# Bias and causal mask of two attentions in 32-key steps and 32-wide blocks, on one Trainium2 core

## What is computed

```python
# layer 0, 16 heads of width 8, 256 queries and keys
buckets = _relative_position_bucket(mem_pos - ctx_pos)   # 0 for keys after the query,
bias = rel_bias[buckets]                                 # up to 31, reached some 30 keys back
scores = einsum('bqhd,bkhd->bhqk', q, k) / sqrt(dh) + transpose(bias, (2, 0, 1))[None]
context = einsum('bhqk,bkhd->bqhd', softmax(scores), v)
# layer 1
att = where(causal, einsum('bthd,bshd->bhts', q, k) / sqrt(D), -inf)
y = einsum('bhts,bshd->bthd', softmax(att), v) @ w_proj + b_proj
```

## Time and profile before

| | us |
|---|---|
| median of the timed runs | 3942.99 |
| profiled execution | 3959.12 |
| its span, first to last instruction | 3956.8 |
| TensorE busy (matmuls) | 3403.3 (86%) |
| VectorE busy | 2900.9 (73%) |
| ScalarE busy | 1902.9 (48%) |
| GpSimd busy | 1549.3 (39%) |
| mean granted TensorE clock | 0.942 |

### The profile page before, as it was taken

One profiled execution on the slowest core, in us unless ns is written; L12 is line 12 of the kernel. 1 busy time (PEld: TensorE's weight loads), 2 busy tenths in 40 slices (PEclk: granted clock), 3 DMA queues, 4 the chain that ended last, 5 costly groups with the idle time before them and its releaser, 6 DMA issues. The chain is left out here.

```text
span 3956.8 us, 60602 instructions
## 1 busy us (share of the span) xinstructions
PE 3403.3 (86%) x20989; PEld 2093.9 (53%) x21044; DVE 2900.9 (73%) x6458; ACT 1902.9 (48%) x3463; POOL 1549.3 (39%) x1015
## 2 busy tenths in 40 slices
PE   5999999878999984677748888888886999999987
PEld 3677776555777762344423333333333666666653
DVE  7888888556777756433239999999997777777765
ACT  2555556324665651222237676776673333333325
POOL 2311111542211200588848877878873011111112
PEclk9999999999999996799869999999998999999998
DMA  6333332004444424233332332322321222222211
GB/s 154 94 89 90 88 89 54 1 5 115 100 101 104 98 62 122 57 44 44 43 78 73 95 100 83 93 78 73 95 79 60 90 87 87 87 87 87 88 59 43
DMA packets 242530, 314.19 MB, mean 79 GB/s; under 512 B 46450, under 2 KB 157779, under 8 KB 231588
## 3 DMA queue, kind: packets, MB, share of 16 engines
q1 hardware_dynamic: 208308, 289.02, 26.3%
q0 software_dynamic: 22528, 17.32, 3.3%
q10 hardware_dynamic: 11392, 3.97, 0.5%
HBM read 251.93 MB, written 57.08 MB: 78 GB/s over the span
## 5 line engine op out<-in xcount | busy, mean ns | idle before, releaser
L574 DVE TENSOR_REDUCE a_Mx<-a_Sx 128x2 f32<-128x512 f32 (+1 forms) x1024 | 590.3, 618 | 172.2 <-PE a_Sx L626 126.7
L2208 POOL TENSOR_TENSOR a_inp<-a_dtu,a_Bs 128x1024 f32<-128x1024 f32 x256 | 597.8, 2359 | 67.9 <-DMA a_Bs<-a_brows 42.5
L2486 DVE TENSOR_TENSOR_SCAN a_h<-a_dA,a_inp 128x1024 f32<-128x1024 f32 x256 | 583.0, 2283 | 31.7 <-ACT a_dA L2369 27.2
L2613 PE MATMUL a_Y<-a_hc,g_ident 128*128 128x512 f32 x1024 | 487.8, 599 | 7.4 <-POOL a_hc L2222 3.5
L347 POOL TENSOR_TENSOR a_rest<-a_qk,a_parts 128x512 f32<-128x512 f32 x64 | 75.2, 1175 | 916.1 <-ACT a_parts L399 916.1
L413 ACT ACTIVATE a_Pr<-a_SA 128x512 f32<-128x512 f32 x512 | 305.4, 596 | 168.6 <-DVE a_SA L524 79.6
L623 PE MATMUL a_Sx<-att_Kp,att_Qp 96*128 96x256 bf16 (+1 forms) x2048 | 345.3, 261 | 42.7 <-DMA att_Qp<-a_crows 17.9
L2369 ACT ACTIVATE a_dA<-a_dtA,a_A 128x512 f32<-128x512 f32 x512 | 329.8, 681 | 97.5 <-DVE a_h L2486 96.5
L1958 ACT ACTIVATE f_sg<-f_GB 128x512 f32<-128x512 f32 x272 | 162.6, 598 | 436.6 <-PE f_GB L2034 436.4
L2084 PEld LDWEIGHTS f_OUT<-g_routed_wd,f_hm 128*128 128x128 f32 x2176 | 280.6, 191 | 123.5 <-issue 90.5
L2613 PEld LDWEIGHTS a_Y<-a_hc,g_ident 128*128 128x128 f32 x1024 | 195.4, 194 | 234.2 <-issue 223.0
(11 more groups left out here) (480 smaller groups left out, 6771.3 us busy)
## 6 DMA issues: line engine op xcount, KB each, us to landing
a_Bs<-a_brows SPq DMA_DIRECT2D x256, 256.0 KB, 3.3
f_Cs<-f_crows SPq DMA_DIRECT2D x512, 128.0 KB, 2.9
att_Qp<-a_packing SPq DMA_DIRECT2D x192, 192.0 KB
att_Kp<-a_packing SPq DMA_DIRECT2D x192, 192.0 KB
a_packing<-a_parts SPq DMA_DIRECT2D x64, 384.0 KB
a_packing<-a_parts SPq DMA_DIRECT2D x64, 128.0 KB
a_Cs<-a_brows SPq DMA_DIRECT2D x32, 256.0 KB, 4.7
g_x<-x SPq DMA_DIRECT2D x8, 512.0 KB, 7.3
```

The source lines that it names most:

```text
L574: nc.vector.tensor_reduce(Mx[(k + 2 - (j < LATE)) % 2][:, t, 2 * jj:2 * jj + 2], Sx[t][:, 0:2 * wd].rearrange("p (h q) -> p h q", h=2), AX ...
L2208: nc.gpsimd.tensor_tensor(inp[n % Q][:], dtu[k][:], Bs[n % Q][:].unsqueeze(1).to_broadcast([P, CH, GT]), ALU.mult).then_inc(s["mulB"], 1)
L2486: nc.vector.tensor_tensor_scan(h[n % 2][:].rearrange("p c q -> p (c q)"), dA[m % 2][:].rearrange("p c q -> p (c q)"), inp[n % Q][:].rearra ...
L2613: nc.tensor.matmul(Y[c][:], ident[:], hc[n % Q][:, c], start=False, stop=(n == N - 1))\
```

## The change

In the first attention the far bias becomes a step per 32 keys: the six constant rows become 24 (eight blocks of 32 keys by three parts), filled straight from the stored lines. What is left of the bias then lies in blocks of 32 queries by 64 keys around the diagonal, and is added at all four places by four matmuls that write 32 partitions each (`fold`, 96 x 32, stationary; `near_q` or `near_k` moving, 128 columns, twice 64 at the border). `add_band`, `band`, `bmax`, `bexp` and their TensorE and VectorE setup go; the lines shrink from 3 x 512 to 768 columns, and all placing moves to SP, ahead of the packing's second half. In the causal attention the 24 rows hold -1e30 for keys in later blocks of 32, and the mask inside a block is added by four matmuls of 2 x 32 columns at each of the four places. Each small matmul increments the semaphore, whose waits count by W = 4. In `choose` four matmuls of 512 columns whose result nobody reads follow the matmul of each of 30 rounds. In `state_space` `spread_C` for n = 3 and 6 is issued one state earlier, ahead of the `Y` matmuls of n = 1 and 4.

```diff
@@ attention, SP @@
+                        if not causal and b == -3:
+                            bias.store(sp)
@@ after the two packing stores of the step @@
+                        if not causal and b == -3:
+                            bias.place(sp)
+                            constants(0, s["consts"])
@@
                     if not causal and b == -3:
-                        bias.store(sp)
-                        constants(0, s["consts"])
                         constants(1, s["consts"])
@@ attention, ScalarE @@
-                            wait(act, s["sa_mm"] if causal else s["biased"], 8 * b + j + 1)
+                            wait(act, s["sa_mm"], W * (8 * b + j + 1))
@@ attention, VectorE @@
-                def add_band(b, j):
-                    v.wait_ge(s["sa_mm"], 8 * b + j + 1)
-                    near = pair(SA[j % 2], K0Q)[:, :, 0:BAND]
-                    nc.vector.tensor_tensor(near, near, band[:, 2 * j:2 * j + 2], ALU.add).then_inc(s["biased"], 1)
@@ attention, TensorE @@
+                def add_mask(both, mask, done):
+                    for r in range(4):
+                        tile = slice(32 * r, 32 * r + 32)
+                        nc.tensor.matmul(both[tile, :, tile], identb[:, tile],
+                                         mask[:, tile].unsqueeze(1).to_broadcast([P, 2, 32]),
+                                         start=False, stop=True).then_inc(done, 1)
@@ maxima @@
                         if causal:
-                            last = nc.tensor.matmul(both[:, :, wd - P:wd], identb[:],
-                                                    maskq[:].unsqueeze(1).to_broadcast([P, 2, P]), start=False, stop=True)
+                            add_mask(both[:, :, wd - P:wd], maskq, s["mx_mm"])
                         else:
-                            last = nc.tensor.matmul(both[:, :, lo:hi], flip[:], bmax[...], start=False, stop=True)
+                            for r in range(4):
+                                q0 = t * P + 32 * r
+                                lo = max(q0 - 32, 0)
+                                nc.tensor.matmul(both[32 * r:32 * r + 32, :, lo:q0 + 32], fold[:],
+                                                 near_q[:, 2 * j:2 * j + 2, lo - q0 + 32:64],
+                                                 start=False, stop=True).then_inc(s["mx_mm"], 1)
+                def add_bias(both, h0, first_key, done):
+                    for r in (3, 0, 1, 2):
+                        q0 = first_key + 32 * r
+                        hi = min(q0 + 64, S)
+                        nc.tensor.matmul(both[32 * r:32 * r + 32, :, q0:hi], fold[:], near_k[:, h0:h0 + 2, 0:hi - q0],
+                                         start=False, stop=True).then_inc(done, 1)
@@ scores_near: add_mask(both[:, :, 0:P], ...) or add_bias(both, h0, 0, s["sa_mm"]); scores_far: @@
-                        for i in range(NPART):
-                            last = nc.tensor.matmul(both[:, :, P:2 * P], flip[:], bexp[:, i, h0:h0 + 2, 0:P],
-                                                    start=False, stop=(i == NPART - 1))
+                        add_bias(both, h0, P, s["sb_mm"])
@@ choose, TensorE, b in range(BITS + 1) @@
+                for i in range(BESIDE if b < BITS else 0):
+                    nc.tensor.matmul(IDLE[:], identb[:], identb[:].unsqueeze(1).to_broadcast([P, BL, P]),
+                                     start=True, stop=True)
@@ state_space, TensorE @@
-                    if on(0) and n < N - 1 and n + 1 not in MOVED:
+                    if on(0) and n < N - 1 and n not in MOVED and n + 1 not in MOVED:
                         spread_C(g * N + (n + 1), n + 1, k)
@@
                         wait_product(pe, g * N + n)
+                        if n + 1 in MOVED:
+                            spread_C(g * N + (n + 2), n + 2, k)
```

More of the change, by code:

```diff
@@ L558, in step @@
                         bb, jj = slot(b, j)
[L559 to L569, removed]
                         if (x_ if j >= LATE else m):
                             for t in range(TB):
-                                wait(v, s["mx_mm"], 16 * bb + (2 * jj + t + 1))
+                                wait(v, s["mx_mm"], W * (16 * bb + (2 * jj + t + 1)))
                                 wd = P * (t + 1) if causal else S
@@ L639, in scores_near @@
                     for u in range(2):
-                        last = nc.tensor.matmul(both[:, u], K[:, h0 + u, 0:P], Q[:, h0 + u, :],
-                                                start=(u == 0), stop=(u == 1 and not causal))
+                        nc.tensor.matmul(both[:, u], K[:, h0 + u, 0:P], Q[:, h0 + u, :],
+                                                start=(u == 0), stop=False)
                     if causal:
-                        last = nc.tensor.matmul(both[:, :, 0:P], identb[:],
-                                                maskk[:].unsqueeze(1).to_broadcast([P, 2, P]), start=False, stop=True)
-                    last.then_inc(s["sa_mm"], 1)
+                        add_mask(both[:, :, 0:P], maskk, s["sa_mm"])
+                    else:
+                        add_bias(both, h0, 0, s["sa_mm"])
                 def scores_far(b, k, j):
@@ L748, in step @@
                             pe.wait_ge(s["thr_ready"], 2)
-                            pe.wait_ge(bias.band_placed, NPART * 16)
-                            for g, hs in enumerate(BANDS):
-                                wait(pe, s["band_ev"], g - 1)
-                                for i in range(NPART):
-                                    last = nc.tensor.matmul(
-                                        SA[g % 2][:, 0:len(hs) * BAND].rearrange("p (h q) -> p h q", q=BAND),
-                                        flip[:], bexp[:, i, hs[0]:hs[-1] + 1, :],
-                                        start=(i == 0), stop=(i == NPART - 1))
-                                last.then_inc(s["band_mm"], 1)
                         if x_ and j == LATE:
@@ L822, in store @@
     def store(self, sp):
[L823 removed]
         sp.wait_ge(self.seq, 5)
[L825 to L828 removed]
+        sp.dma_start(self.lines.rearrange("i h n -> h i n"), self.lparts[:]).then_inc(self.stored, 16)
     def place(self, eng):
@@ L840, in look_up @@
     def look_up(self, pe):
         pe.wait_ge(self.loaded, 32)
-        for i in range(3):
-            self.nc.tensor.matmul(self.LP[i], self.rel[:], self.hot[:, i, :], start=True, stop=True)\
-                .then_inc(self.made, 1)
+        for out, cols in self.LP:
+            self.nc.tensor.matmul(out, self.rel[:], self.hot[:, cols], start=True, stop=True).then_inc(self.made, 1)
     def copy_lines(self, act):
-        N, line = self.N, self.line
-        act.wait_ge(self.made, 3)
-        for i in range(3):
-            self.nc.scalar.activation(line[:, i * N:i * N + N], self.LP[i], ACT.Copy).then_inc(self.got, 1)
+        act.wait_ge(self.made, 2)
@@ L2651, in l1_attn @@
     norm_factors(nc, res, "n2")
-    attention(nc, res, "a2", {"zrows": a["c_zrows"]}, True, res["held"])
+    attention(nc, res, "a2", {"later": a["c_later"]}, True, res["held"])
 def l0_ffn(nc, res, a):
```

130 lines of the change are left out of this document (57 added, 73 removed).

## The result

| | before | after |
|---|---|---|
| median of the timed runs, us | 3943.31 (4 runs) | 4117.01 (4 runs, 4113.69 to 4117.43) |
| profiled execution / its span, us | 3959.12 / 3956.8 | 4117.43 / 4115.2 |
| busy: TensorE / VectorE / ScalarE, us | 3403.3 / 2900.9 / 1902.9 | 3627.0 / 2809.4 / 1925.6 |
| a batch, first / causal attention, us | 19.71 / 17.30 | 22.23 / 20.36 |

The change makes the kernel slower: ratio 1.044, 95% interval 1.0421 to 1.0458, or +174 us.

What follows compares the result with a forecast made beforehand. The prediction took TensorE's stream to bound both attentions. First attention +75, causal +89, start-up -16, search -5 and recurrence 0 made +143 us, put on the 3943.0 median: 4086 us, range 4025 to 4165.

Steps and rivals of the forecast that it cites:

- The bound: Both attentions: TensorE's stream sets the time, busy 541 of 555 us and 466 of 480; relieving VectorE is worth little.
- The price of a layout change: Small groups in both attentions: 0.095 us each way, so a group costs 0.265 us in the first, 0.24 in the second.
- A batch: Attention batches grow by 2.35 us in the first and 2.78 in the second; times 32, +75 and +89 us.
- What TensorE's gaps gave back: Waits in TensorE's stream that the longer stream fills: 0.8 us recovered a batch in the first attention.
- Start-up: Before the first attention's scores: the expanded-bias wait and band making go (14 us), -16 us in all (-22 to -6).
- the first is shorter too: Start-up: TensorE's 17.9 us wait for the constant rows, until 44.55, was also to become shorter.
- The search: Search for the k-th score: four idle matmuls a round lift the clock from 0.50, -5 us (-9 to +10).
- The recurrence: Earlier spread of C for n = 3 and 6: gain eaten by a later wait, 0 us (+3 to -15).
- (a): Rival on the attentions' small groups: no layout price, -151 us, some 3800 us in total; chance 0.10.
- (b): Rival on the attentions' small groups: half the layout price, 85 us less in each stage, about 3935 us; chance 0.05.
- (c): Rival on TensorE in the attentions: granted clock falls to 0.95, adding 67 us, 4155 us in total; chance 0.08.
- (d): Rival on the small matmuls: they run one after the other, adding 170 and 90 us, about 4350 us; chance 0.04.

Runs made afterwards that it cites:

- two-trips run: Changed kernel, reordered so that TensorE enters the small-matmul layout twice a pair of heads instead of four times; 3947.36 us, ratio 1.0008 to the kernel before.
- warm start: Changed kernel plus seventy idle 512-column matmuls on TensorE ahead of its wait for the constant rows; 4120.87 us, ratio 1.0456 to the kernel before.
- run `ordinary`: Changed kernel with each small group as four ordinary matmuls, stationary operands zero-padded to 128 columns; 3988.69 us, ratio 1.0113 to the kernel before.

## Why the prediction came out as it did

It said 4086 us and a range of 4025 to 4165; 4117 is inside it, 31 above the forecast. Step by step:

- **The bound.** Right. TensorE's stream sets the length of a batch; 3.9 us less work for VectorE a batch bought nothing beyond the gaps.
- **The price of a layout change.** Right. It forecast 0.20 in and 0.15 out, a group at 0.265 and 0.24; the trace has 0.202 and 0.161 (0.135 for 64 columns), a group at 0.263 and 0.237. That the price is for changing the layout and not for the small matmuls is shown by the two-trips run. What the prediction did not have: the second ordinary matmul behind a group starts 0.119 after the first in place of 0.109. With 32 groups that is 0.3 us a batch.
- **A batch.** +2.35 forecast, +2.53 measured; +2.78 forecast, +3.06 measured. The 0.3 above covers both differences. What TensorE's gaps gave back, taken as the remainder, was right in size: in the first attention 3.13 + 0.32 - 2.53 = 0.9 us (0.8 forecast), in the causal one 3.43 + 0.32 - 0.1 (the groups being 0.003 cheaper each) - 3.06 = 0.6 (0.65 forecast). Times 32: +81 and +98 for +75 and +89, so 15 us of the miss.
- **Start-up.** Wrong, the largest single miss: -16 forecast (-22 to -6), some -4 measured. Up to the ternary layer the changed kernel is 77 us behind the first profile of the kernel before, 75 behind the later one, and 32 batches make 81. The band and its wait did go. The first scores of the kernel before, then TensorE in the changed kernel:

```profile
76.56 0.60 PE L640 MATMUL a_SA<-att_Qp,att_Kp 128*128 128x256 bf16 x4
```

```profile
45.96 0.61 PE L614 MATMUL a_Sx<-att_Kp,att_Qp 96*128 96x256 bf16 x2 [19.71 <-DMA att_Qp<-a_lines]
...
71.02 0.61 PE L639 MATMUL a_SA<-att_Qp,att_Kp 128*128 128x256 bf16 x2
...
81.86 0.59 PE L614 MATMUL a_Sx<-att_Kp,att_Qp 96*128 96x256 bf16 x2
82.37 0.24 PE L622 MATMUL a_Sx<-a_near_q,a_fold 96*32 96x64 bf16 x4
82.55 0.39 PE L614 MATMUL a_Sx<-att_Kp,att_Qp 96*128 96x256 bf16 x2
```

  The first maxima start at 45.96 for 44.55: the wait is longer (19.71 for 17.90), not shorter, and it is a DMA that fills the `Qp` rows from the lines. And the maxima that follow run at half speed, two of 256 columns in 0.61 us for 0.39, until 82 us. The kernel before is at half speed to 48.7 us and again, while it mostly waits for the expanded bias, from 58.9 to 69.2. So the first scores come at 71.02 for 76.56, 5.5 us earlier and not 15, and the batch that they begin lasts 25.6 us for 18.9, 6.7 longer, where a steady one is 2.5 longer. The two failed steps are "the first is shorter too" and the unstated assumption that what follows runs at full speed.

  What the half speed costs was to be shown by the warm start, which could not hold the clock. The run `ordinary` tells more. It has the same sums and the same constant rows, and its clock rises at 53.4 us:

```profile
53.40:63.60 10.20, 8.45 (x83) 6.01 (x82) 9.23 (x17) 2.23 (x5) 3.46 (x3) 1.00 0.61 105
63.60:67.00 3.40, 3.40 (x24) 2.83 (x22) 2.54 (x6) 1.28 (x1) 0.00 (x0) 0.50 0.57 159
67.00:82.00 15.00, 14.89 (x198) 12.47 (x197) 9.71 (x21) 8.84 (x18) 3.44 (x3) 1.00 0.50 115
```

  Its first scores start at 67.98, and its ternary layer 38.5 us later than before, where 32 batches, 1.50 longer each, make 48: its start-up is shorter by 9.5 us, against 4 in the changed kernel. That puts the half speed at some 5 us, an estimate, for layout changes in the filling batches are in it too; 6 or 7 us of the forecast's 16 are missing even there. In all seven profiles with the small groups in the first attention these matmuls come to full speed between 79.7 and 87.7 us, in the six without them by 53.4 (with one spell at 0.50 after it). So the long half speed comes with the small groups; how they keep the clock low is open.
- **The search.** -5 forecast; from the first to the last count 5.5 less in the changed kernel and alone; a round takes 1.75 us for 1.95 once the clock has risen.
- **The recurrence.** 0 forecast; from the first scan to the last 946.2 us for 947.0 (944.1 and 944.9 in the other profiles of the kernel before), and 1.000 alone.
- **The sum.** +81 + 98 - 4 - 5.5 = +169 for the measured +174 (+171 between profiles of like expert-choice layers). Putting the forecast's difference on the median, and not on the profiled execution's 3959, was right; its 16 us above the median lay for 10 us in the expert-choice layer.
- **The rivals.** (a) no layout price: excluded by the rows above. By the Trainium skill's page "TensorE: Matmul & The Clock Gate", section "Packing small matmuls — row/col tiling", the small matmuls start about 4 ns apart, and the trace agrees with 3. It doesn't charge the coming and going: 28 more entries and exits a batch, at 0.093 + 0.106, are 5.6 us, more than the whole loss of 2.5 or 3.1. (b) half the price: excluded by 0.202 and 0.161 together. (c) a lower clock: 1.00 in both windows; it was low in the start-up alone. (d) in series: 0.003 from one to the next.

Of the signs that it named, those for the distances (0.15 and 0.20), the batches (22 and 20), and the search's clock (0.95, above 0.9) came, and TensorE's gaps shrank; VectorE's share fell to 66% and not to 60%; the first scores came 5.5 us earlier and not 15.

## What to carry to other kernels

Count the changes of TensorE's tile layout before the columns: each costs some 0.09 us in and 0.10 out, together the time of some 450 columns of ordinary streaming (256 in 0.109), so a group of small matmuls side by side pays only if it replaces more than that and its own stream, or if several groups share one trip. Where the order allows it, gather the ordinary matmuls of several results first and then all their small ones: that alone took 4.1% off the changed kernel. And take a change apart: under this one's loss of 4.4% lay blocks that bring a gain of 0.6%, once the first attention makes two trips, the causal one keeps its old mask, and the search its idle matmuls (0.1% by themselves).

## What the hardware showed beyond that

- Ordinary bf16 matmuls of 128 columns with a new 128-column stationary operand each follow one another every 0.055 us, those of 64 columns every 0.028: the weight loads hide even there.
- A group directly behind another in the same 32-column layout starts 0.03 or 0.056 us after the last matmul of the one ahead (both are frequent in the two-trips run), in another output bank.
- After 14 us of uninterrupted 512-column matmuls at full speed and an idle time of 3.35 us, the clock stayed at 0.50 for 40.9 us, in which TensorE was busy for 39.4. With four ordinary matmuls in place of each small group it had risen by 53.4 us.
- In the changed kernel's profile the same stretch is printed with clock 1.00 although its matmuls take 0.61 us for 0.39. Such a reading is to be held against the length of a known matmul.
- The expert-choice layer's gathers took 370 or 381 us with the same code, the same within each set of runs on one chip, and single batches at the start of a stage differ by up to 9 us between executions.
